# Order of dense and gathered experts, and of the router's plan, in a two-layer graph network with mixtures of experts

## The reference

```python
gate_out = x @ gate_w + routing_bias                 # 16 experts
top_v, top_i = jax.lax.top_k(gate_out, K)            # K = 4 for each token
weights = softmax over the chosen experts, 0 elsewhere
out = _swiglu(x, sw1, sw2, sw3)                      # shared expert, all tokens
for e in range(E):
    out = out + _swiglu(x, w1[e], w2[e], w3[e]) * weights[..., e:e + 1]
return x + out
```

## Time and profile before

| | us |
|---|---|
| median of 3 runs (lowest, highest) | 527.73 (526.92, 528.93) |
| the profiled execution | 531.01 |
| its span, first to last instruction | 529.2 |
| PE busy | 493.8 (93%) |
| PEld busy | 308.8 (58%) |
| DVE busy | 273.7 (52%) |
| ACT busy | 206.7 (39%) |
| moved by DMA | 191.05 MB, mean 361 GB/s |

### The profile page before, as it was taken

One profiled execution on the slowest core, in us unless ns is written; L12 is line 12 of the kernel. 1 busy time (PEld: TensorE's weight loads), 2 busy tenths in 40 slices (PEclk: granted clock), 3 DMA queues, 4 the chain that ended last, 5 costly groups with the idle time before them and its releaser, 6 DMA issues.

```text
span 529.2 us, 6662 instructions
## 1 busy us (share of the span) xinstructions
PE 493.8 (93%) x2576; PEld 308.8 (58%) x2576; DVE 273.7 (52%) x324; ACT 206.7 (39%) x227; POOL 9.1 (2%) x46
## 2 busy tenths in 40 slices
PE   7999899999969849999999999999999999969987
PEld 4664344366856626666756756656655636526665
DVE  6734510167895463475367357547438015563483
ACT  1111000057752445446255255355454023444441
POOL 2000000010000000000000000000000000000000
PEclk9998999999979969999999999999999999979998
DMA  8999999999957639999999999999999999999640
GB/s 340 422 420 421 422 419 422 418 409 418 415 225 292 211 107 328 380 416 386 373 416 418 361 417 414 363 415 417 377 410 416 406 383 364 417 410 346 228 201 20
DMA packets 37555, 191.05 MB, mean 361 GB/s; under 512 B 4218, under 2 KB 4602, under 8 KB 32148
## 3 DMA queue, kind: packets, MB, share of 16 engines
q1 hardware_dynamic: 37328, 190.48, 91.5%
q10 hardware_dynamic: 196, 0.14, 0.1%
HBM read 190.35 MB, written 0.26 MB: 360 GB/s over the span
## 4 chain that ended last, share of the span: by engine, by line
PE 75%; DMA 11%; DVE 10%; ACT 2%; issue 2%; POOL 0%; SPq 0%; ACTq 0%; DVEq 0%; POOLq 0%
PE ps L1705 14%; PE ps L1691 13%; PE ps L1747 12%; PE ps L1760 7%; DMA w_raw<-in_w 6%; PE ps L1695 6%; DMA wv_sb<-in_wv 5%; PE ps L1339 3%; PE ps L1727 3%; DVE s_lo L982 2%; PE ps L1503 2%; DVE s_lo L968 2%; DVE h L1166 2%; PE ps L1520 1%; PE ps L1332 1%
## 5 line engine op out<-in xcount | busy, mean ns | idle before, releaser
L968 DVE TENSOR_TENSOR s_lo<-w_raw,s_hi 128x1365 fp32r<-128x1365 f32 x72 | 111.3, 1578 | 55.4 <-ACT s_hi L708 54.9
L708 ACT CAST s_hi<-w_raw 128x1365 fp32r<-128x1365 f32 x72 | 94.0, 1334 | 21.5 <-DMA w_raw<-in_w 16.7
L1691 PE MATMUL ps<-s_hi,xT_hi 128*128 128x512 f32 (+2 forms) x216 | 88.1, 408 | 7.0 <-DVE s_lo L968 7.0
L1705 PE MATMUL ps<-w_raw,exS 128*64 128x512 f32 (+1 forms) x512 | 84.3, 471 | 0.0
L1691 PE MATMUL ps<-s_lo,xT_hi 128*128 128x512 f32 (+2 forms) x216 | 80.4, 374 | 0.0
L982 DVE TENSOR_TENSOR s_lo<-w_raw,s_hi 128x1536 fp32r<-128x1536 f32 (+1 forms) x36 | 58.1, 1622 | 20.6 <-ACT s_hi L721 19.8
L721 ACT CAST s_hi<-w_raw 128x1536 fp32r<-128x1536 f32 (+1 forms) x36 | 48.9, 1370 | 45.2 <-DMA w_raw<-in_w 40.1
L1705 PEld LDWEIGHTS ps<-w_raw,exS 128*64 128x64 f32 x512 | 35.5, 140 | 47.7 <-issue 47.7
L1691 PEld LDWEIGHTS ps<-s_hi,xT_hi 128*128 128x128 f32 x216 | 41.3, 191 | 28.0 <-issue 11.6
L1695 PE MATMUL ps<-s_hi,xT_lo 128*128 128x512 f32 (+2 forms) x216 | 56.9, 372 | 0.0
L1691 PEld LDWEIGHTS ps<-s_lo,xT_hi 128*128 128x128 f32 x216 | 41.4, 192 | 8.5 <-issue 1.9
(11 more groups left out here) (293 smaller groups left out, 457.8 us busy)
## 6 DMA issues: line engine op xcount, KB each, us to landing
w_raw<-in_w SPq DMA_DIRECT2D x128, 682.5 KB, 9.8
w_set<-in_w SPq DMA_DIRECT2D x31, 1024.0 KB, 26.1
w_raw<-in_w SPq DMA_DIRECT2D x27, 768.0 KB, 8.8
w_raw<-in_w3s SPq DMA_DIRECT2D x24, 768.0 KB, 9.9
w_raw<-in_sw SPq DMA_DIRECT2D x8, 682.5 KB, 15.6
w_raw<-in_w SPq DMA_DIRECT2D x9, 512.0 KB, 9.5
wk_sb<-in_wk SPq DMA_DIRECT2D x2, 1024.0 KB, 16.7
wq_sb<-in_wq SPq DMA_DIRECT2D x2, 1024.0 KB, 15.9
```

The costliest lines, as they stand in the source:

```text
L708: a.copy(s_hi[pair_of(g)][:, 0:F1], raw[:, 0:F1]).then_inc(hi_ready, 1)
L968: v.tensor_tensor(s_lo[pair][:, 0:F1], raw[:, 0:F1], s_hi[pair][:, 0:F1].bitcast(F32), ALU.subtract).then_inc(lo_ready, 1)
L1691: mm(bank(i + c0 // D)[:, 0:n], xT_hi[:, k], w[:, c0:c0 + n], start=(k == 0 and w is hi), stop=False)
L1705: last = mm(bank(NC * part + c0 // D)[FEW * g:FEW * g + FEW, 0:n], exS[:, k, tokens], w[:, CW * g + c0:CW * g + c0 + n], start=(k == 0), s ...
```

## The change

1. `KINDS` becomes DDSDSDSDSDSDSDSDS: dense and gathered experts alternate to the end, and the last is gathered, not dense.
2. The end is rewritten for that: the last gathered expert's down product is made in two halves of 256 columns (banks 7 and 6), each half of y is copied and spread by a product of its own (banks 0 and 1), then added to x3. x3 is added to bank 6 earlier, behind the dense expert 15's down product.
3. VectorE: `router` is cut in `choose` (ranks) and `routed_gates`; `plan_tokens` loses its last step to `plan_gates`. All are put in other places among the casts of experts 0 and 1. `copy_y` goes behind a second low part of w2.
4. ScalarE: the copies of the gathers go behind casts of w2(1), the fourth behind a cast of expert 1's down matrix; the copies of the spread matrices behind all of expert 1's and the silu of expert 2.
5. TensorE: each gather follows a w2 product of expert 1; the spread products go among expert 1's down products; `add_few` goes one product later.

```diff
-KINDS = "DD" + "SD" * 5 + "SSDSD"
+KINDS = "DD" + "SD" * 7 + "S"
-    last_halves = [half_bank(7), half_bank(0)]
+    last_halves = [half_bank(7), half_bank(6)]
+    sum_halves = [half_bank(0), half_bank(1)]
@@ scalar
-            a.activation(xn[:], x3[:], ACT.Copy, scale=rstd[:]).then_inc(rows_ready, 1)
             hi_w3(0, 0)
             hi_w3(0, 1)
             hi_w3(0, 2)
             hT_to_hi(0, 0)
             hi_w3(0, 3)
             hT_to_hi(0, 1)
-            copy_gathered(0)
+            a.activation(xn[:], x3[:], ACT.Copy, scale=rstd[:]).then_inc(rows_ready, 1)
             hT_to_hi(0, 2)
-            copy_gathered(1)
             hi_w2(1, 0)
             hi_w2(1, 1)
-            copy_gathered(2)
             silu(1)
             hi_w2(1, 2)
-            copy_gathered(3)
+            copy_gathered(0)
             hi_w2(1, 3)
-            copy_spread(0)
+            copy_gathered(1)
+            copy_gathered(2)
 
             def end_full(e):
 
                 hi_w3(e, 0)
+                if e == 1:
+                    copy_gathered(3)
...
                 else:
+                    end_full(m - 1)
+                    silu_few(m)
                     if m == 2:
+                        copy_spread(0)
                         copy_spread(1)
...
-            end_full(NE - 1)
+            copy_hTS(NE - 1, 0)
+            copy_hTS(NE - 1, 1)
@@ vector
-            router()
+            choose()
+            lo_w1(1, 2)
             gated(0)
+            lo_w1(1, 3)
             plan_order()
-            lo_w1(1, 2)
-            lo_w1(1, 3)
             lo_w3(0, 0)
             hT_to_lo(0, 0)
-            plan_tokens()
             lo_w3(0, 1)
             lo_w3(0, 2)
             hT_to_lo(0, 1)
             lo_w3(0, 3)
             hT_to_lo(0, 2)
-            for k in range(KT):
+            routed_gates()
+            lo_w2(1, 0)
+            plan_tokens()
+            for k in range(1, KT):
                 lo_w2(1, k)
+            plan_gates()
...
                     lo_w2(m, 0)
+                    lo_w2(m, 1)
                     copy_y(m - 1)
-                    for k in range(1, KT):
-                        lo_w2(m, k)
+                    lo_w2(m, 2)
+                    lo_w2(m, 3)
...
             last = NE - 1
-            end_full(last)
-            dve.wait_ge(used, unit_w3(last, W3_UNITS - 2) + 1)
-            then(v.scalar_tensor_tensor(x3[:], bank(6), minus_mean3, x3[:], ALU.subtract, ALU.add))
+            dve.wait_ge(used, unit_w3(last - 1, W3_UNITS - 1) + 1)
+            v.scalar_tensor_tensor(x3[:], bank(6), minus_mean3, x3[:], ALU.subtract, ALU.add).then_inc(x3_ready, 1)
+            gated_few(last)
             for b in range(2):
                 dve.wait_ge(last_ps, b + 1)
-                v.tensor_tensor(xn[:, HALF[b]], last_halves[b], x3[:, HALF[b]], ALU.add).then_inc(out_ready, 1)
+                v.tensor_copy(y_sb[:, HALF[b]], last_halves[b]).then_inc(y_few_ready, 1)
+            for b in range(2):
+                dve.wait_ge(sum_ps, b + 1)
+                v.tensor_tensor(xn[:, HALF[b]], sum_halves[b], x3[:, HALF[b]], ALU.add).then_inc(out_ready, 1)
@@ tensor
-                if m == 2:
-                    spread_few(1)
...
-                    if m == 1 and u > 0:
-                        gather_few(u - 1)
+                    if m == 2 and u in (0, 2):
+                        spread_few(u // 2)
                 for k in range(KT):
                     up_part(m, 1, k)
-                    if m == 1 and k == 0:
-                        gather_few(KT - 1)
-                    if m == 1 and k == 2:
-                        spread_few(0)
-                    if m == 2 and k == 0:
-                        pe.wait_ge(round_ready, KT)
-                    if k == 1 and m > 0 and not is_full(m - 1):
+                    if m == 1:
+                        gather_few(k)
+                    if k == 2 and m > 0 and not is_full(m - 1):
                         add_few(m - 1)
+                if m == 1:
+                    pe.wait_ge(round_ready, KT)
...
+            for b in range(2):
+                for i in range(HALVES * S_TILES):
...
+                    last = mm(last_halves[b][own], hTS[0:rows, t, own], w3_raw[0:rows, i, HALF[b]], start=(t == 0), stop=(t == S_TILES - 1),
+                              skip_group_check=True)
                 last.then_inc(last_ps, 1)
+            for b in range(2):
+                pe.wait_ge(y_few_ready, few_no(last_e) + 1 + b)
+                mm(sum_halves[b], spread[:, few_no(last_e)], y_sb[:, HALF[b]], start=True, stop=True).then_inc(sum_ps, 1)
```

More of the change, by code:

```diff
@@ L365, in gps_kernel @@
     hT_ps, hT_hi_ready, hT_lo_ready = sem("hT_ps"), sem("hT_hi_ready"), sem("hT_lo_ready")
-    last_ps, out_ready, out_stored = sem("last_ps"), sem("out_ready"), sem("out_stored")
+    last_ps, sum_ps, out_ready, out_stored = sem("last_ps"), sem("sum_ps"), sem("out_ready"), sem("out_stored")
+    x3_ready = sem("x3_ready")
     N_CONSTS = 7
@@ L1195, in router_max, with choose @@
                 v.tensor_scalar(small[:, 0:1], small[:, 2:3], -1.0, None, ALU.mult).then_inc(negmax1_ready, 1)
-            def router():
+            def choose():
                 other = logits1[:].unsqueeze(1).to_broadcast([P, E1, E1])
@@ L1205, in router, with routed_gates @@
                 v.tensor_scalar(chosen[:], rank1[:], float(K1), None, ALU.is_lt).then_inc(chosen_ready, 1)
+            def routed_gates():
                 dve.wait_ge(exp1_ready, 1)
+                dve.wait_ge(chosen_ready, 1)
                 w = weights1[:, 1:1 + E1]
@@ L1244, in plan_tokens, with plan_gates @@
                                        position_at[:].unsqueeze(2).to_broadcast(each), ALU.add, ALU.is_equal).then_inc(hots_ready, 1)
+            def plan_gates():
+                each, own = [P, len(SPARSE), FEW], slice(BUSY, E1 - 1)
                 dve.wait_ge(hots_ready, 1)
@@ L1745, in down @@
                         first = e == 0 and t == 0 and a is hT_hi and w is s_hi
-                        final = e == NE - 1 and u == W3_UNITS - 2 and i == n - 1 and a is hT_lo
+                        final = e == NE - 2 and u == W3_UNITS - 1 and i == n - 1 and a is hT_lo
                         last = mm(bank(6), a[0:rows, t], w[pair][0:rows, D * i:D * i + D], start=first, stop=final)
@@ L1827, in _ @@
-                    if k == 1 and m > 0 and not is_full(m - 1):
+                    if m == 1:
+                        gather_few(k)
+                    if k == 2 and m > 0 and not is_full(m - 1):
                         add_few(m - 1)
+                if m == 1:
+                    pe.wait_ge(round_ready, KT)
             last_e = NE - 1
-            for c in range(NC):
+            for c in range(len(S_HT)):
                 transpose_h(last_e, c)
-            for u in range(W3_UNITS - 1):
-                down(last_e, u)
@@ L1836, in _ @@
-            u = W3_UNITS - 1
-            pe.wait_ge(lo_ready, unit_w3(last_e, u) + 1)
-            pe.wait_ge(hT_lo_ready, NC * len(FULL))
-            pair = pair_of(unit_w3(last_e, u))
-            t0, n = DOWN[u]
-            for b in range(2):
-                for i in range(n):
-                    rows = LAST_ROWS if t0 + i == FT - 1 else P
-                    for a, w in ((hT_hi, s_hi), (hT_hi, s_lo), (hT_lo, s_hi)):
-                        last = mm(last_halves[b], a[0:rows, t0 + i], w[pair][0:rows, D * i + D // 2 * b:D * i + D // 2 * b + D // 2],
-                                  start=(i == 0 and a is hT_hi and w is s_hi), stop=(i == n - 1 and a is hT_lo))
+            pe.wait_ge(x3_ready, 1)
@@ new lines, in _ @@
+            for b in range(2):
+                for i in range(HALVES * S_TILES):
+                    t, g = i // HALVES, i % HALVES
+                    if b == 0:
+                        if i % 3 == 0:
+                            pe.wait_ge(ld_down[i // 3], down_loads(last_e, i // 3))
+                        if i == 0:
+                            pe.wait_ge(y_few_ready, few_no(last_e))
+                        if g == 0 and t in (0, KT):
+                            pe.wait_ge(hTS_ready, len(S_HT) * few_no(last_e) + t // KT + 1)
+                    rows, own = P if t < S_TILES - 1 else S_LAST, slice(FEW * g, FEW * g + FEW)
+                    last = mm(last_halves[b][own], hTS[0:rows, t, own], w3_raw[0:rows, i, HALF[b]], start=(t == 0), stop=(t == S_TILES - 1),
+                              skip_group_check=True)
```

8 lines of the change are left out of this document (4 added, 4 removed).

## The result

| | before | after |
|---|---|---|
| median, run in turn on one chip (lowest, highest of after) | 528.33 | 509.13 (509.09, 510.26) |
| ratio, 95% interval | | 0.9634 [0.959, 0.9679] |
| the profiled execution | 531.01 | 510.26 |
| its span | 529.2 | 508.5 |
| PE busy | 493.8 (93%) | 485.1 (95%) |

The kernel is 19.2 us faster by the medians, 3.7%. The same bytes are moved at a higher mean rate: what went is dead time of the queue. TensorE's busy time fell by 8.7 us although it does nearly the same products: before, its clock stood at half for longer (the PEclk rows).

The account below looks back on a forecast made before the run. It took the DMA queue and TensorE as both full in the steady part, with queue time lost in the front and a tail. Front 11.6 plus order and tail 9.9 make 21.5; 527.73 - 21.5 = 506.2 us, range 500.5 to 516.5.

Parts of the forecast that it names:

- the slow tail: Rival, at the end: last product at 1.2 GHz or with bare weight loads, 5 us more, about 511; chance 0.13.
- the rule: Last product: weight loads overlap only across row groups, so 24 more loads add 3.3 us, giving 509.5; chance 0.05.
- the steady part: Alternating pairs from expert 3 on: 41.96 us each, unchanged; moving the y copy gains 0, bound 2 us.
- Front: Up to dense expert 3: it starts at 201.8 instead of 213.41, saving 11.6 us, bounds 8 to 14.
- half of the 2.45 us of half clock: Front, behind TensorE's 2.3 us wait for h of expert 1: 1.2 us added for a clock that may fall.
- the later table: Front: the table gating expert 2's load comes 1.4 us later, a price paid in full as dead queue.
- the rival in which TensorE sets the pace: Steady part: with the queue ahead, the y wait counts, 2 us less, 504; chance 0.07.
- I take 0, since the queue is full: Steady part: removing TensorE's small wait around the y copy, 0.3 us a pair, gains nothing; bound 7 x 0.3 = 2.
- Order and tail: Late run: strict alternation avoids starving and the tail is rewritten; end at 519.3 against 529.2, saving 9.9 us.
- 1.0 for the clock: Tail: 1.0 us added for a clock that may fall in gaps with only transposes between; bounds 0 and 5.9.
- six listed terms: Tail after 507.1: gate to copy with handovers 2.2, last product 5.5, copy 0.42, spread 0.45, add 0.42, store 2.1; given as 11.2.
- Signs named beforehand: Profile marks listed for right (expert 3 near 202, queue share above 0.75) or wrong (a pair over 42.5 us).

Follow-up runs that it names:

- `front_only`: The kernel before with only the front's moves (casts, plan, gathers, spread copies; old expert order, tail and y copy): 517.47 us, ratio 0.979.
- `y_back_load128`: The kernel after with the y copy at its old place and each gathered expert's last down-matrix tile on 128 partitions, not 48: 509.33 us, ratio 0.9633.
- `load128`: The kernel after with the last tile of each gathered expert's down matrix loaded on 128 partitions, zero-filled, instead of 48: 505.77 us, ratio 0.9561.
- `table_early`: The kernel after with the order of experts computed before the low part of tile 3 of w1(1), not behind it: 509.51 us, ratio 0.9654.
- `before_load128`: The kernel before with the last tile of each gathered expert's down matrix loaded on 128 partitions instead of 48: 525.28 us, ratio 0.9939.
- `tail_only`: The kernel before with only the new order of experts and new tail; old front and place of the y copy: 521.42 us, ratio 0.9865.

## Why the prediction was right, and where it was off

**506.2 was forecast, 509.13 measured**, inside the range and faster, as forecast. The number alone lies nearer to both values of the slow tail (509.5 by the rule, 511) than to the forecast; what tells them apart is the profile, in which the tail is not slow. What was right is front, order and tail. What was off is the baseline, and one term of the steady part came out only because two errors cancelled.

**Front: right in size and cause.** Expert 3's start was put at 201.8. It is at 202.93, in an execution that reached the mixture 0.87 us later than the profile of before (first product of expert 0 at 129.97 against 129.10): 202.1 on the same footing. Its links held as well: expert 2 starts at 177.43 (176.7 forecast, 177.6 with the 0.87), the wait for h is 2.19 (2.3). `front_only` measured 11.6, forecast 11.6. One link was a guess: half of the 2.45 us of half clock. The clock did fall behind the 2.19 us wait here (0.57 from 183 to 187). Six more kernels of this study have the same front and the same wait (2.18 or 2.19), and of their profiles only that of `y_back_load128` shows the fall. In `load128`:

```profile
181.59 0.66 PE L1742 MATMUL ps<-ident,h 128*128 128x128 f32 x4 [2.19 <-DVE h L1166]
```

the clock is 1.00 from 181.5 to 186. From the first product of expert 0 to the start of expert 3 it is 84.31 us before, 72.9 or 73.0 in the two profiles with the fall, and 71.4 or 71.5 in the five without. The fall costs 1.6, not 2.45, and the front's gain is 11.4 with it and 12.9 without. That the guess hit the median is luck. The queue's 15.1 MB over this part were read rightly, but the later table was not the price it was called (`table_early`).

**Steady part: the sum right, for another reason.** Seven pairs take 293.45 us, 41.92 each; 41.96 less nothing was forecast, since the queue is full. In fact three pairs took 41.3, by the rival in which TensorE sets the pace, until the queue's arrears showed, and the other four 41.86 to 42.87. The step "I take 0, since the queue is full" is the one whose reason failed: the wait around the copy of y was worth 0.5 us a pair, not 0.3, and before it was TensorE that set most of the 41.96 (`y_back_load128`, `before_load128`). That its removal came to nothing is luck: the queue took back in four pairs what three had won. The rival's 504 is what `load128` comes near to, once the queue is faster. What the prediction read as one bound, share 1.01 and TensorE busy in 177.04 of 178.20, was two paces 2% apart, and 397 GB/s was not the queue's full rate. The sign was on the page: the chain's pieces of 9.33 and 9.39 us in two ordinary pairs, which the prediction passed over.

**Order and tail: the size off.** 519.3 was forecast for the span without the front's gain, and `tail_only` has 519.3, in an execution that reached the mixture 0.8 us later. The second matrix of the last gathered expert ends at 491.61 + 4.77 = 496.38; forecast were 507.1 - 11.6 + 0.87 = 496.4. The tail is 12.1, forecast 12.2 with 1.0 for the clock (its six listed terms add up to 11.1, not to the 11.2 it gives). The clock stayed at 1.00, and the microsecond went into 0.3 of the halved product, two adds in 0.95 in place of one in 0.42, and longer handovers. But the gain is against the kernel before, and there 9.9 was forecast, 7.7 measured [5.2 to 9.1 by the ratio's interval].

**The step that cost the 2.9 us is the first one:** "The runs' median is 527.73, 0.6% lower; I subtract the saving from that." The saving was worked out on one execution of 531.01 us, above all three runs then shown. Against that execution the forecast was 509.5 and the measured one 510.26, of which 0.87 is the later start. Against the median it was 2.9 too low: 3.28 that the profiled execution of before lies above its median, less the 1.13 of after, plus that 0.76. Of the 33 executions of before beside the later runs one is longer than 531.01; their median is 528.9, so the 527.73 of the first three was also 1.2 low. Why that execution was a long one is not shown, as no other of this kernel was profiled. The granted clock points to it: its mean is 0.977 in the eleven shortest of the 33 and 0.971 in the eleven longest, and 0.971 in the profiled one, which has 6.8 us of half clock at the starved place where the profile of `front_only` has 3.4. If so, the tail's term carried it: the starved stretch cost more in that execution than in most.

**The weight-load rule.** The last product with 48 matmuls of 256 columns takes 5.85 us, with 24 of 512 it takes 5.52: 0.3 for 24 more loads of 136 ns, not 3.3. By the Trainium skill, TensorE: Matmul & The Clock Gate, Part 3, a weight load overlaps running matmuls only where the row groups differ, so these loads would stand bare; the trace does not bear that out for these 64-column weights. The same page's Part 4 says that transposes don't count as busy for the clock in the same way. No run here shows an effect: with idles of 1.02 and 0.55 us around six transposes the granted clock was 1.00.

**Signs named beforehand.** Expert 3's start, the wait for h, no transfer in front of the last product, the last low part 25 us before the end and the 12 us from the last exS product came true. Two missed narrowly: the queue's share from 148 to 200 is 0.72, not above 0.75, and one transfer in the chain has 10.06 us, just over 10. And one sign of being wrong came true: a pair over 42.5 us, the fifth with 42.87. The last two are the queue's arrears, the part of the mechanism that the prediction had wrong.

## What to carry to other kernels

If two resources both look full, they may be two paces a per cent or two apart, and the slower one hides part of what an edit to the other gives: either edit alone moved the median by 1.0 or 0.8 us here, both by 4.4. Look at the single pairs in the profile, and measure both edits together before dropping either. And work a saving out against the execution it was read from, then carry it to the median only with the difference between the two as part of the range. Work that waits for an input belongs behind work that doesn't, on every engine that works in order: the copies and spreads behind the casts gave 6 us, the gate ahead of the low parts took 6.5 back.

## What the runs showed of the hardware

- While a tile of 192 KB onto 48 partitions is under way, the whole queue slows: 332 GB/s over 7 us around it (288 and 271 from 368 to 372), 304 with 256 KB on 64 partitions, 417 with 512 KB on 128. The DMA share shows 1.02 or 1.03 in all three, so only the GB/s column tells. The median time from issue to landing of all 682.5 KB tiles of w1 and w2 is 9.8, 10.6 and 8.7 us with 48, 64 and 128. In a kernel that lives at the queue's pace this decided 6.5 us one way and 3.4 the other.
- Behind the same wait of TensorE (2.18 or 2.19 us) at the same place the granted clock fell in two of seven profiles (0.57 from 183 to 187 in the kernel after, 0.58 in `y_back_load128`) and stayed at 1.00 in five. The fall costs 1.6 us up to the start of expert 3. A plan should carry both outcomes.
- Halving the width of matmuls with 64-column weights cost 0.3 us for 24 more weight loads: the loads lay beside the matmuls.
